# Self-attention of a decoder layer: three score steps a head group, low output parts on GpSimd, one output projection inside the second attention

## What is computed

```python
q, k, v = hidden @ Wq.T, hidden @ Wk.T, hidden @ Wv.T   # 16 heads of 32
q, k = layer_norm(q * gamma + beta), layer_norm(k * gamma + beta)
attn = jnp.einsum('bqhd,bkhd->bhqk', q * D ** (-0.5), k) ** 2
attn = jnp.where(mask, attn, 0.0)                       # causal
o = jnp.einsum('bhqk,bkhd->bqhd', attn, v)
z = jnp.sum(attn, axis=-1)
o = o / (z + EPS)
return o @ Wo.T
```

## Time and profile before

| | us |
|---|---|
| median of 3 runs | 1251.58 |
| lowest and highest run | 1249.16, 1252.71 |
| the profiled execution | 1257.09 |
| its span | 1255.4 |

### The profile page before, as it was taken

How to read it: one execution, slowest core, us unless ns; L and a number is a source line. 1 busy time by engine, 2 the same in 40 slices (tenths; PEclk the granted TensorE clock), 3 DMA queues, 4 the chain that set the end, 5 groups by cost and what they waited for, 6 DMA issues and landing times. The chain is left out here.

```text
span 1255.4 us, 21905 instructions
## 1 busy us (share of the span) xinstructions
PE 1012.5 (81%) x8049; PEld 682.5 (54%) x8049; DVE 856.6 (68%) x1409; ACT 708.0 (56%) x1078; POOL 236.7 (19%) x208
## 2 busy tenths in 40 slices
PE   4988988799647677777777777777679989999997
PEld 3743734688436444444444444444557756565565
DVE  6757726899698699999999999999560521111225
ACT  2355352355516799999999999999223201122210
POOL 1124033565460200000000000000533620000022
PEclk9989989899869699999999999999779999999998
DMA  8200001310000100000000000000030395132124
GB/s 322 88 1 1 1 1 68 118 45 22 9 1 1 43 2 2 2 0 0 0 0 0 0 0 0 0 0 0 1 149 26 122 381 230 67 118 68 54 86 145
DMA packets 24854, 68.14 MB, mean 54 GB/s; under 512 B 2722, under 2 KB 6818, under 8 KB 23778
## 3 DMA queue, kind: packets, MB, share of 16 engines
q1 hardware_dynamic: 20114, 52.48, 11.2%
q0 software_dynamic: 4400, 14.42, 3.6%
q10 hardware_dynamic: 288, 0.52, 0.1%
HBM read 49.07 MB, written 18.35 MB: 54 GB/s over the span
## 5 line engine op out<-in xcount | busy, mean ns | idle before, releaser
L1278 DVE TENSOR_REDUCE cs_top<-cs_s_b 128x1 f32<-128x512 f32 x256 | 164.7, 685 | 17.9 <-PE cs_s_b L1307 8.7
L1315 PE MATMUL cs_tp<-ident,cs_p_int 128*128 128x128 f16 x2048 | 159.1, 221 | 7.3 <-ACT cs_pT L1258 2.6
L1252 ACT ACTIVATE cs_p_int<-cs_s_b,cs_bias,cs_step_now 128x1024 int16<-128x1024 f32 x128 | 154.2, 1205 | 12.4 <-DVE cs_bias L1285 5.3
L1266 DVE TENSOR_REDUCE cs_top<-cs_s_a 128x1 f32<-128x1024 f32 x128 | 155.5, 1215 | 7.5 <-PE cs_s_a L1307 7.5
L1315 PEld LDWEIGHTS cs_tp<-ident,cs_p_int 128*128 128x128 f16 x2048 | 122.6, 98 | 60.3 <-issue 46.1
L1307 PE MATMUL cs_s_b<-k_parts,q_int 96*128 96x512 bf16 x256 | 79.3, 392 | 94.0 <-ACT cs_p_int L1252 93.7
L1252 ACT ACTIVATE cs_p_int<-cs_s_a,cs_bias,cs_step_now 128x1024 int16<-128x1024 f32 x128 | 152.9, 1194 | 0.0
L1258 ACT CAST cs_pT<-cs_tp 128x1024 bf16<-128x1024 int16 x128 | 129.6, 1012 | 3.9 <-PE cs_tp L1315 3.3
L2124 PE MATMUL ff_h<-ff_experts,ff_zgT 128*128 x368 | 112.9, 460 | 0.9 <-ACT ff_zgT L1763 0.9
L1411 POOL TENSOR_TENSOR co_o<-co_o,v_step 128x512 f32<-128x512 f32 x8 | 10.6, 1331 | 470.1 <-DVE co_o L1433 470.1
L1307 PE MATMUL cs_s_a<-k_parts,q_int 96*128 96x512 bf16 x256 | 79.8, 395 | 22.7 <-ACT cs_p_int L1252 18.3
(11 more groups left out here) (270 smaller groups left out, 2111.9 us busy)
## 6 DMA issues: line engine op xcount, KB each, us to landing
ff_experts<-in_experts_dram SPq DMA_DIRECT2D x8, 2176.0 KB, 14.9
slots<-sa_zero SPq DMA_DIRECT2D x1, 5888.0 KB, 24.6
ff_zg<-slots POOLq DMA_DIRECT2D x23, 256.0 KB, 2.9
run_y<-ff_yv SPq DMA_DIRECT2D x23, 256.0 KB, 2.0
ff_raw<-in_weights_dram SPq DMA_DIRECT2D x6, 768.0 KB, 6.0
ck_raw<-in_ctxT_dram SPq DMA_DIRECT2D x8, 512.0 KB, 3.4
stage<-in_cwkv_dram SPq DMA_DIRECT2D x2, 1024.0 KB, 6.2
out_dram<-x_res SPq DMA_DIRECT2D x8, 256.0 KB, 2.0
```

What stands on the lines that cost most here:

```text
L1252: nc.scalar.activation(p_int[:, u, half * HALF:(half + 1) * HALF], s[:, :], ACT.Exp, bias=bias[:, u:u + 1], scale=step_now[:, h:h + 1], ac ...
L1266: nc.vector.tensor_reduce(top[:, u, 0:1], s_a[u][:, :], AX_X, ALU.max).then_inc(max_ok, 1)
L1278: nc.vector.tensor_reduce(top[:, u, 1 + c:2 + c], s_b[:, c * 512:(c + 1) * 512], AX_X, ALU.max).then_inc(max_ok, 1)
L1315: ins = nc.tensor.transpose(tp[:, k, :], p_int[:, u, key:key + P].bitcast(F16), ident16[:, :])
```

## The change

- Key tiles 2 and 3 of a group share one bank for each head: the scores of key tile 2 go into columns 0 to 255 of it and those of key tile 3 into columns 256 to 383. A group has three parts instead of four steps; ACT squares the third in one instruction of 384 columns. The masks stay one instruction for each key tile, four a group; both masks of the third part wait for all of its squares. PE's order stays two steps ahead: scores of step s+2, values of step s, the third part's values being those of both key tiles.
- `low_out` moves from DVE to POOL, behind the masks of the next group; `divide` waits for it before it writes `o32` again.
- For tile 4 the square of the features stands behind the first group's squares, and the roots behind `high_out(0)`; `variances(4)` stands between `take_sums(0)` and `divide(0)`, and `finish_features(4)` behind `divide(1)`. ACT no longer waits for `wo_lo_ok` ahead of the first squares.
- The output projection of tile 3 goes into bank `num` and stands after the first two score steps of the second attention; the first of these wait for only three tiles to be added, and the third for all four.

```diff
+PARTS = 3
...
-        STEPS = HG * BT
+        STEPS = HG * PARTS
+        def part_of(kt):
+            return min(kt, PARTS - 1)
+        def cols_of(kt):
+            return slice(0, 2 * P) if kt == 2 else slice(2 * P, 3 * P) if kt == 3 else slice(kt * P, S)
+        def spread(kt, j):
+            return att[:, part_of(kt), j, cols_of(kt)]
...
+        def out_bank(n):
+            return num if n == BT - 1 else sc[n % BT]
...
-            sp.wait_ge(av_ok, B * STEPS)
+            sp.wait_ge(av_ok, B * HG * BT)
...
-            def mask_step(step):
-                kt = step % BT
-                diag = att[:, kt, :, kt * P:(kt + 1) * P]
-                pool.wait_ge(att_ok, (step + 1) * GH)
+            def mask_tile(n, kt):
+                diag = att[:, part_of(kt), :, cols_of(kt).start:cols_of(kt).start + P]
+                pool.wait_ge(att_ok, (n * PARTS + part_of(kt) + 1) * GH)
...
+            def low_out(n):
+                pool.wait_ge(ohi_ok, n + 1)
+                pool.tensor_tensor(oT_lo[:, n % HG, :], o32[:, :], oT_hi[:, n % HG, :].bitcast(F32),
+                                   ALU.subtract).then_inc(olo_ok, 1)
...
-            for step in range(B * STEPS):
-                mask_step(step)
+            for n in range(B * HG):
+                if n == HG:
+                    low_out(n - 1)
+                for kt in range(BT):
+                    mask_tile(n, kt)
+                if n % HG:
+                    low_out(n - 1)
+            low_out(B * HG - 1)
...
-            def roots(n):
+            def square_features(n):
...
+            def roots(n):
...
-            def squares(b, hg):
-                for kt in range(BT):
-                    step = b * STEPS + hg * BT + kt
-                    if hg or b:
-                        act.wait_ge(av_ok, step - BT + 1)
+            def squares(n):
+                for part in range(PARTS):
+                    if n:
+                        act.wait_ge(av_ok, (n - 1) * BT + (BT if part == PARTS - 1 else part + 1))
+                    cols = slice(part * P, S) if part < PARTS - 1 else slice(0, 3 * P)
...
-                        use = step * GH + j
+                        use = (n * PARTS + part) * GH + j
...
-                        nc.scalar.activation(att[:, kt, j, kt * P:S], ring[use % RING][:, kt * P:S],
-                                             ACT.Square).then_inc(att_ok, 1)
+                        nc.scalar.activation(att[:, part, j, cols], ring[use % RING][:, cols], ACT.Square).then_inc(att_ok, 1)
...
-            for n in range(5):
+            for n in range(4):
...
+                square_features(n)
...
-            act.wait_ge(wo_lo_ok, CK)
-            for hg in range(HG):
-                squares(0, hg)
-                if hg:
-                    high_out(hg - 1)
+            read_z(5)
+            read_v(4)
+            read_qkT(3)
+            squares(0)
+            square_features(4)
+            squares(1)
+            high_out(0)
+            roots(4)
+            squares(2)
+            high_out(1)
+            squares(3)
+            high_out(2)
...
-            high_out(HG - 1)
+            high_out(3)
...
+            square_features(5)
...
+            square_features(6)
...
+            square_features(7)
...
-            for hg in range(HG):
-                squares(1, hg)
-                if hg:
-                    high_out(HG + hg - 1)
+            for n in range(HG, 2 * HG):
+                squares(n)
+                if n > HG:
+                    high_out(n - 1)
...
             def divide(n):
...
+                if n:
+                    v_.wait_ge(olo_ok, n)
...
-            def low_out(n):
-                v_.wait_ge(ohi_ok, n + 1)
-                nc.vector.tensor_tensor(oT_lo[:, n % HG, :], o32[:, :], oT_hi[:, n % HG, :].bitcast(F32),
-                                        ALU.subtract).then_inc(olo_ok, 1)
             def add_out(n):
...
-                nc.vector.tensor_tensor(x_res[:, n, :], x_res[:, n, :], sc[n % BT][:, :], ALU.add).then_inc(out_read, 1)
+                nc.vector.tensor_tensor(x_res[:, n, :], x_res[:, n, :], out_bank(n)[:, :], ALU.add).then_inc(out_read, 1)
...
-                variances(n)
+                if n < 4:
+                    variances(n)
+            take_sums(0)
+            variances(4)
+            divide(0)
+            take_sums(1)
+            divide(1)
...
-            take_sums(0)
-            divide(0)
-            for hg in range(1, HG):
-                take_sums(hg)
-                low_out(hg - 1)
-                if hg < HG - 1:
-                    divide(hg)
+            take_sums(2)
+            divide(2)
+            take_sums(3)
...
-            low_out(HG - 1)
...
             for n in range(BT):
...
-            for hg in range(HG):
-                take_sums(HG + hg)
-                if hg:
-                    low_out(HG + hg - 1)
-                divide(HG + hg)
-            low_out(2 * HG - 1)
+            for n in range(HG, 2 * HG):
+                take_sums(n)
+                divide(n)
...
-            def scores(b, s):
-                hg, kt = s // BT, s % BT
-                step = b * STEPS + s
+            def scores(step):
+                n, part = step // PARTS, step % PARTS
+                hg = n % HG
...
-                for j in range(GH):
-                    rows = slice(D * j, D * (j + 1))
-                    nc.tensor.matmul(ring[(step * GH + j) % RING][:, kt * P:S], kT[rows, hg, kt * P:(kt + 1) * P],
-                                     qT[rows, hg, kt * P:S], start=True, stop=True,
-                                     tile_position=(D * j, 0)).then_inc(s_ok, 1)
-            def values(b, s):
-                hg, kt = s // BT, s % BT
-                step = b * STEPS + s
-                if kt == 0 and hg:
-                    pe.wait_ge(nd_read, 2 * (b * HG + hg))
-                pe.wait_ge(masked, step + 1)
-                for j in range(GH):
-                    rows = slice(D * j, D * (j + 1))
-                    nc.tensor.matmul(num[rows, kt * P:S], v[:, b * BT + kt, (hg * GH + j) * D:(hg * GH + j + 1) * D],
-                                     att[:, kt, j, kt * P:S], start=(kt == 0), stop=(kt == BT - 1))
-                for j in range(GH):
-                    rows = slice(D * j, D * (j + 1))
-                    ins = nc.tensor.matmul(den[rows, kt * P:S], ones[:, :], att[:, kt, j, kt * P:S],
-                                           start=(kt == 0), stop=(kt == BT - 1))
-                    if j == GH - 1:
-                        ins.then_inc(av_ok, 1)
+                for kt in ((0,), (1,), (2, 3))[part]:
+                    for j in range(GH):
+                        rows = slice(D * j, D * (j + 1))
+                        ins = nc.tensor.matmul(ring[(step * GH + j) % RING][:, cols_of(kt)],
+                                               kT[rows, hg, kt * P:(kt + 1) * P], qT[rows, hg, kt * P:S],
+                                               start=True, stop=True, tile_position=(D * j, 0))
+                        if kt != 2:
+                            ins.then_inc(s_ok, 1)
+            def values(step):
+                n, part = step // PARTS, step % PARTS
+                b, hg = n // HG, n % HG
+                if part == 0 and hg:
+                    pe.wait_ge(nd_read, 2 * n)
+                for kt in ((0,), (1,), (2, 3))[part]:
+                    pe.wait_ge(masked, n * BT + kt + 1)
+                    for j in range(GH):
+                        rows = slice(D * j, D * (j + 1))
+                        nc.tensor.matmul(num[rows, kt * P:S], v[:, b * BT + kt, (hg * GH + j) * D:(hg * GH + j + 1) * D],
+                                         spread(kt, j), start=(kt == 0), stop=(kt == BT - 1))
+                    for j in range(GH):
+                        rows = slice(D * j, D * (j + 1))
+                        ins = nc.tensor.matmul(den[rows, kt * P:S], ones[:, :], spread(kt, j),
+                                               start=(kt == 0), stop=(kt == BT - 1))
+                    ins.then_inc(av_ok, 1)
             def attention(b, tiles):
+                first, end = b * STEPS, (b + 1) * STEPS
...
-                    pe.wait_ge(out_read, BT)
-                scores(b, 0)
-                scores(b, 1)
+                    pe.wait_ge(out_read, BT - 1)
+                scores(first)
+                scores(first + 1)
...
-                for s in range(STEPS):
-                    if s + 2 < STEPS:
-                        scores(b, s + 2)
-                    values(b, s)
+                if b:
+                    output(BT - 1, range(HG))
+                    pe.wait_ge(out_read, BT)
+                for step in range(first, end):
+                    if step + 2 < end:
+                        scores(step + 2)
+                    values(step)
             def output(n, groups):
...
```

(4 more changed lines are left out.)

## The result

| | before | after |
|---|---|---|
| median of seven runs each, us | 1251.20 | 1244.05 |
| lowest and highest | 1249.16, 1252.71 | 1243.56, 1247.11 |
| the profiled execution; its span | 1257.09; 1255.4 | 1247.11; 1245.4 |

The ratio after / before is 0.995, with a 95% interval of 0.9937 to 0.9963: 4.6 to 7.9 us less. Two later comparisons of the same code, each on another chip with runs of before beside it, gave 0.9946 and 0.9939. I had forecast 1251.0 and a range of 1245.5 to 1257. The result is faster by more than 0.3%, and the median lies 1.45 us under the range: **the prediction was wrong**.

A forecast was written before the change was run, and what follows sets the result against it. Steady groups were taken as bound by the chain sums, reciprocal, product, high part, two squares. Terms -3.1+0.1+0.4+1.8+1.4-1.2+0.1+1.1 gave 0.6 us gained, so 1251.6 - 0.6 = 1251.0 us, range 1245.5 to 1257.

The forecast's parts named there:

- the second start: Second attention up to group 4's sums, T(4): tile 3's projection leaves the path, clock falls; 1.4 us gained (0.3 to 3.4).
- rival A: Clock stays up in the two starts or group 0's wait, product slips past masks: some 1246 us; chance 0.26.
- The wait for `add_out(3)`: Second attention, ahead of the third scores: PE waits for this addition, 0.9 us.
- The first start: First attention up to group 0's sums, T(0): squares start earlier, clock falls; 1.8 us gained, 3.9 if it stays up.
- Group 0: Sums of group 0 to group 1, T(0) to T(1): variances and roots delay it, clock falls; 3.1 us lost.
- Steady groups: Between sums' starts: T(1) to T(2) 10.17 us for 10.23, T(4) to T(5) 1.2 lost, T(5) to T(6) 0.1 gained.
- PE's matmuls stay as they are: Shared bank, each group: PE's matmuls are unchanged; only where PE has to wait counts.
- The last group of a batch: End of the first batch: 128-column scores leave PE's way and the ending chain is 0.44 us shorter; 0.4 us gained.
- Tail: Last sums to output projections: low part on POOL starts at T+6.6, ends at T+7.9; 1.1 us gained, clock falls.
- B: Rival: clock falls in every steady group behind its 1.9 us wait, 6.0 us in all: 1257 us; chance 0.16.
- C: Rival: low parts on POOL cost what they are longer by, 4.9 us: 1255.9 us; chance 0.02.
- D: Rival: the shared bank does nothing, as ACT is not the bound; if starts gain nothing either, 1253 us; chance 0.04.

The follow-up runs named there:

- low_pool: Kernel before with only the low parts moved from DVE to POOL: 0.9983 (0.9964 to 1.0001), -2.1 us.
- `both`: Changed kernel with high parts behind the first part of the next squares, and variances ahead of the first sums, roots ahead of these squares: 1235.92 us, 0.986.
- after_again: Changed kernel unchanged, run again for a second profile: 0.9946 (0.9929 to 0.9962).
- variances_first: Changed kernel with tile 4's variances ahead of the first sums and its roots ahead of the first high part: 0.9916 (0.9889 to 0.9944).
- bank_alone: Kernel before with only the shared bank and its three parts: 0.9992 (0.9973 to 1.0012), -1.0 us.
- after_third: Changed kernel unchanged, third profile, on another chip: 0.9939 (0.9921 to 0.9957).
- after_low_dve: Changed kernel with the low parts back on DVE, between sums and reciprocal: 0.9954 (0.993 to 0.9978).
- filler: Kernel before with matmuls of no use put into PE's waits of both attention starts, nothing removed: 0.9946 (0.992 to 0.9971), -6.8 us.
- features_late: Kernel before with only tile 4's features and roots behind the first squares: 0.9976 (0.9959 to 0.9994), -3.0 us.
- out_inside: Kernel before with only tile 3's output projection inside the second attention: 0.9986 (0.9968 to 1.0004), -1.8 us.
- high_later: Changed kernel with each high part on ACT behind the first part of the next group's squares: 0.9877 (0.9839 to 0.9914), -15.5 us against before.

## Why the prediction was wrong

The step that failed most is that the clock falls in the second start: it stayed at 1.00 in all three profiles of after, and the term measured 3.3 us instead of 1.4. What decides whether it falls stays open.

**The second start.** This is the largest mis-sized term: 1.4 us forecast, 3.3 measured in all three profiles of after (2.70 by T(3) to the second S, 0.63 behind it). The first half was right: the projection's 2.8 us leave the path. What failed is the step "it runs at the fallen clock for some 3 us (+1.4 us)". The clock stayed at 1.00, and T(4) came 16.5 us after the transposes (1.76 as in rows 5, and 14.72) instead of 18.8. It is at the bound of 3.4 us that I had named, by the mechanism of rival A; what the clock gave (2.7 us, from 15.35 to low_pool's 12.66) the projection took back. The size of the step was right: in `both`, where the clock did fall, the stage is 1.54 us longer. So it failed in whether the clock falls, which these runs do not explain. Even with the fallen clock T(4) comes 18.0 us after the transposes, so 0.8 us of the 18.8 were too much elsewhere; 0.6 of these may be the shared bank's (15.36 to 14.72), which I had named only for the last groups. The wait for `add_out(3)` was there (0.78 us at 166.21), at about its forecast size of 0.9.

**The first start.** 1.8 forecast, 3.1, 4.7 and 3.1 measured. "The second batch before had just that start, and the clock fell there; I take it to fall here too" was half right: in after_again it did not fall, in the other two it came down later and for a shorter time, which costs 1.6 us (13.5 for 11.91). With the clock up I had put 3.9, and it was 4.7. The wait itself was as worked out: second scores 2.30 us after the first, where I had put 2.3.

**Group 0.** T(0) to T(1): 12.8 forecast (9.71 and 3.1), 12.92, 12.56 and 12.35 measured. The wait is 2.71 us for 3.0, and the clock falls behind it, as taken. variances_first shows the cause: with the wait at 1.57 us the 2.6 us are gone. The size was forecast right here.

**Steady groups.** 10.17 forecast for T(1), T(4) and T(5), 9.77, 9.77 and 9.76 measured, apart from the first profile's 11.99. What failed for the larger part is the meeting of product and mask: I had the masks end at T+5.3 and the product at T+5.9; the third part's squares start 0.87 us after T instead of 1.1, the masks end at T+5.09 and the product, which begins at T+4.71, at T+5.64. The 0.5 us that the product was to lose to the mask were 0.24, and the scores come at T+7.33 for T+7.6. The other 0.14 us lie behind them (2.43 us to the next T for 2.57). "PE's matmuls stay as they are" did not hold by the profile: PE is busy for 7.65 us in such a group instead of 8.07, in bank_alone too, and for 8.07 in low_pool, so it comes with the shared bank. The direction held: group 4 loses (0.79 for 1.2), all of it by the shared bank (9.77 in bank_alone), and group 5 gains (0.47 for 0.1).

**The last group of a batch.** T(2) to T(3) gave 1.1 us instead of 0.4. I had counted only the 0.44 us of 128-column scores. bank_alone gives just that (6.63 us for 7.07), but with the clock low at its start; low_pool gives 0.38 by itself (6.69), which I had left out. The trace shows why: from T(2) to T(3) before, DVE is busy without a gap (low part at 114.05 for 1.77 us, reciprocal, product until 119.81, T(3) at 119.92), while in low_pool it is idle for 0.22 us ahead of T(3). PE's own work is not moved by this: its transposes start 6.54 us after T(2) before and 6.55 in low_pool, but 5.79 in after_third and 5.78 in after_low_dve. So PE's part, 0.75 us, comes with the bank: the 0.44, a wait for the last mask (it ended at 118.77, and PE's last values began at 118.82), and a rest of 0.1 or so.

**Tail.** 1.1 forecast, 1.3 measured: the low part begins at T+6.38 and ends at T+7.64. But the forecast put this down to the low part, and low_pool gives only 0.50 of it alone, since its product meets a mask there (1.76 us); bank_alone gives 0.63. That the number fits is in part luck. "The clock falls as before" held: behind 1.93 us it is at 0.59 in the first four us, and the projections take 14.39 us.

**The rivals.** A was the nearest: the clock stays up, here in one start of two (in after_again in both) and not behind group 0, and the product slips past the masks for the most part. I gave it 0.26, because the only row with the same waits had a low clock. Its 5.6 us (the whole gain, not "more") hold one term of 1.5 us, where my own sums had two of that size, the clock behind group 0's wait and the three masks; with both it is 7.1 us and 1244.5, so the range did not reach as far as its own rival. B did not come in after: the steady wait is 1.56 us instead of 1.9, and the clock is 1.00 behind it from T(4) to T(6) in all three profiles. Its mechanism is real all the same: in bank_alone the clock fell behind both steady waits of 2.0 us, and in the first profile of after behind one of 2.03, though in after_low_dve it stayed up behind one of 2.01. C did not come: low_pool is not slower although each low part takes 1.26 us on GpSimd, against the 0.68 of the fastest and 0.90 of after_low_dve's. The Trainium skill's rule of "GPSIMD Engine Reference", section "Engine selection", holds for the duration (1.26 against 0.68 us), not for the kernel. D falls with filler and the parts: the starts gain. (Its 1253 should have been 1254.2, the sum without 1.8 and 1.4.)

**The size of the miss.** Against after_third the terms were off by 1.3 (first start), 0.5 (group 0), 0.4 and 0.7 (T(1), T(2)), 1.9 (second start), 0.4 and 0.4 (T(4), T(5)) and 0.2 (tail), all in the same direction, 5.8 us together. The median lies 6.95 us under the forecast; the last 1.2 us are in no stage of this table. Where I had to choose, I had mostly taken the clock low or the mask met, or left an effect out. The range came from the same choices, and so ended 1.45 us too early. The two largest misses, 1.9 and 1.3 us, lie in the two starts, where the clock did not do what I had taken.

## What to carry to other kernels

Where the lower clock stands behind a short wait, measure first what it costs: a few matmuls of no use in the wait, into a bank that is free, took 5.3 us off two starts here with nothing removed (0.9946 in all, as much as a change in four parts). Where an engine stands in its written order at a step whose result nobody needs soon (ACT at the high part, 3.16 us a group), move that step behind the next piece of work on the path; this gave 6.9 us by the stages, and 9.95 by the medians, on top of the change. If several unknown terms of a forecast are each taken at their careful end, the sum isn't careful but biased.

## What the runs showed of the hardware that I had not expected

- The clock isn't settled by the wait in front of the scores. Waits of 0.72 to 0.73 and 1.21 to 1.22 us stand in the second start of every kernel but filler, ahead of the first and the second scores; in both profiles of before, in features_late and in `both` the clock is then at 0.50, in all three of after, bank_alone, low_pool, out_inside, high_later, variances_first and after_low_dve it stays up. The wait of 2.48 or 2.49 us ahead of the output projections is followed by 0.55 before and by 1.00 in filler and in out_inside. Behind 2.01 to 2.03 us it fell three times and stayed up once. No run here separates what decides it. Behind 2.71 us it fell in all three profiles of after and in after_low_dve, behind 1.56 to 1.58 us in the steady groups in none.
- The low clock behind short waits costs 5.3 us in the two starts and 1.5 in the output projections, 6.8 us of 1251 by the stages. Each of the four parts differs from before by 1.0 to 3.0 us.
- A product that a mask on POOL delays can be cured by being late: with a low part of 0.90 us ahead of it, it ran in 0.69 instead of 0.93 us, and with the variances ahead of it (features_late) in 0.75 instead of 1.75.
